# Flamingo block with experts and butterflies: full-precision products for the shared expert and the last projections, in place of split operands

## The chip, the cores and the metric

The kernel runs on one core of a Trainium2 chip. The metric is the device time of one execution in microseconds (us). The engines of the core are named as in the profile: PE (TensorE; PEld is its weight load), ACT (ScalarE), DVE (VectorE), POOL (GpSimd) and SP (SyncE, which here only issues transfers).

## The reference

Four residual layers on x, 4 x 1024 tokens of 256 features, float32. Each reads a layer norm of x and adds tanh(gate) times its result.

```python
x = x + tanh(g_xattn[0]) * cross_attention(layernorm(x), ctx, Wq, Wk, Wv, Wo)   # 16 heads, stablemax
x = x + tanh(g_ffn[0])   * experts(layernorm(x), ...)
x = x + tanh(g_xattn[1]) * attention(layernorm(x), ctx, ctx)                    # 16 heads, softmax
x = x + tanh(g_ffn[1])   * butterfly_ffn(layernorm(x), ...)

# experts: 64 experts, top 8 of each token, and one shared expert that every token takes
gu = x @ shared_gate_up_w                                  # 256 -> 2 * 512
shared = silu(gu[:, :512]) * gu[:, 512:] @ shared_down_w   # 512 -> 256
shared = shared * sigmoid(x @ shared_gate_w)
...

# butterfly_ffn
h = x @ W_exp + b_exp                                      # 256 -> 1024
h = butterfly(h, up_weights)                               # 10 stages, linear
h = gelu(h + up_bias)
h = butterfly(h, down_weights)                             # 10 stages, linear
y = h @ W_con + b_con                                      # 1024 -> 256
```

## The kernel before

The tokens are taken in 8 halves of 512 (four tiles of 128). The program has three stages with a meeting of all engines between them. What each engine does, and in which order, comes from one list of units per stage (`plan_first`, `plan_experts`, `plan_last`); every engine walks the whole list and runs the part of each unit that it has, in that order and no other. Semaphores tie the parts together.

Stage 1 is the first attention with the router. It writes the normalised features of each half to DRAM (`feats_scratch`).

Stage 2 is `plan_experts` (line 240). It has a phase that builds the lists of tokens (32 tiles: DVE and ACT make one-hot rows in `hots`, PE sums them in `place`, L803), then a loop of 69 iterations over 64 experts: POOL gathers the tokens of expert n, PE turns those of n-3 (L817), makes gate and up of n-4 (L827) and down of n-5 (L836), and POOL scatters the result (L1663). Two side streams are fed in one step at a time. `fusing`, two steps per iteration, multiplies the butterfly stages into the weights before and behind them (L786, and `across`, which is 8 wide operations each of ACT and DVE, L1078 and L1445). `back` is the shared expert: one step after every second tile from tile 5 on (14 steps), three behind the list phase, and one per iteration where n is no multiple of 8. A half of the shared expert is nine steps (`shared_steps`, line 212): load, split, four `sh_up` blocks with `sh_inner` beside them, a last `sh_inner`, two `sh_down` blocks. The first half has a tenth step, `sh_weights`.

Stage 3 is `plan_last`: the second attention of half h, beside it the softmax peaks of half h+1 (L856, L858, L1532) and the last layer of half h-1. This last layer comes in two bursts a half (`burst`, line 281): four `up` blocks (L908) with peaks between them, then four `out` blocks (L921), one per chunk of attention.

The shared expert and the last layer's two products are made of reduced-precision products (type fp32r), as many as a float32 needs: each operand is split into a rounded high part and a low part that is what is left, and three products are summed in PSUM: high x high, low x high, high x low (`PRODUCTS`). The splits are made by ACT (a copy that rounds) and DVE (a subtraction): of the weights once (`sh_weights`, `split_up`, `split_con`), of the features once a half (`sh_split`, `turn_f`), of the shared expert's inner values in each block (`sh_inner`, L1050 and L1416). The last layer's hidden values are rounded by DVE (L1580) and their rest is made by POOL (L1682). All other products of the kernel on float32 tiles, such as L628, L705, L827, L836 and L786, are single full-precision matmuls.

Of the kernel before, what the change touches and what calls it, by code (L numbers as in the profile page):

```python
# [8 lines left out]
F32 = mybir.dt.float32  # L9
F32R = mybir.dt.float32r  # L10
# [3 lines left out]
ALU = mybir.AluOpType  # L14
# [41 lines left out]
PRODUCTS = ((0, 0), (1, 0), (0, 1))  # L56
# [277 lines left out]
def plan_last():  # L334
# [5 lines left out]
    splits = [("split_up", q) for q in range(0, HB, 2)] + [("split_con", q) for q in (0, 4)]  # L340
# [4 lines left out]
    plan += [("peaks", 0)] + splits + [("scores1", 0)]  # L345
# [31 lines left out]
def build(nc, D, out):  # L377
    ctx = ExitStack()
    with ctx:
# [31 lines left out]
        with ExitStack() as scope:  # L411
            w_con = sb("w_con_fused", [P, HB, DIM], F32, scope)
        con_lo = sb("w_con_low", [P, HB, DIM], F32R)
# [47 lines left out]
        with ExitStack() as scope:  # L461
            w_up = sb("w_up_fused", [P, CD, HID], F32, scope)
        up_lo = sb("w_up_low", [P, CD, HID], F32R)
        hid_bias = sb("hidden_bias", [P, HB], F32)
        b_out = sb("bias_out", [P, DIM], F32)
        with ExitStack() as scope:
# [20 lines left out]
            w_sgu = s1("w_shared_up", [P, 2, CD * 2 * SHARED], F32R)  # L487
            w_sd = s1("w_shared_down", [P, 2, SK * DIM], F32R)
            sh_feats = s1("feats_m", [P, CD * HALF], F32)
            sh_parts = s1("feat_parts", [P, 2, CD * HALF], F32R)  # L490
            sh_silu = [s1(f"shared_silu{i}", [P, HALF], F32) for i in range(3)]
            sh_inner = s1("shared_inner", [P, 2, SK, HALF], F32R)
# [8 lines left out]
            staging = bf_v[:, :, :].rearrange("p a n -> p (a n)")  # L501


        with ExitStack() as scope:
            s2 = lambda n, s, d: sb(n, s, d, scope)
            up_hi = s2("w_up_high", [P, CD, HID], F32R)
            con_hi = s2("w_con_high", [P, HB, DIM], F32R)
            up_parts, con_parts = (up_hi, up_lo), (con_hi, con_lo)
# [13 lines left out]
            feats = s2("feats3", [P, 2, CD, HALF], F32R)  # L522
            hidden = [s2(f"hidden{i}", [P, 2, HALF], F32R) for i in range(BURST)]
            whole = [s2(f"hidden_whole{i}", [P, HALF], F32) for i in range(2)]
# [10 lines left out]
        sh_in, sd_in, con_in, expert_in = sem("sh_in"), sem("sd_in"), sem("con_in"), sems("expert_in", 8)  # L535
# [4 lines left out]
        pool_set, ln_var, ln_rstd, x_biased, x_added, out_biased, hid_split = (  # L540
            sem(n) for n in ("pool_set", "ln_var", "ln_rstd", "x_biased", "x_added", "out_biased", "hid_split"))
# [6 lines left out]
        sh_split, sh_mult, sh_inner_set, matrix_set, across_set = (  # L548
            sem(n) for n in ("sh_split", "sh_mult", "sh_inner_set", "matrix_set", "across_set"))
        x_first, x_att, hid_cast, con_split, out_added = (  # L550
            sem(n) for n in ("x_first", "x_att", "hid_cast", "con_split", "out_added"))
# [3 lines left out]
        feats_set, hot_a_set, got_turned, silu_set, sh_silu_set, sh_rounded, part_set, across_own = (  # L555
            sem(n) for n in ("feats_set", "hot_a_set", "got_turned", "silu_set", "sh_silu_set", "sh_rounded", "part_set", "across_own"))
# [17 lines left out]
        def tensor_program(T):  # L574
# [181 lines left out]
            def sh_down(h, two):  # L756
                key = ("sh_down", h, two)
                if two == 0:
                    T.wait_ge(sh_inner_set, SK * (h + 1))
                    if h == 0:  # L760
                        T.wait_ge(sh_split, 4)
# [1257 lines left out]
```

## Time and profile before

| | before |
|---|---|
| median of 3 runs | 1429.22 us (1424.58 to 1436.71) |
| the profiled execution | 1429.54 us |
| its span | 1427.9 us |
| mean granted PE clock | 0.891 |
| busy: PE, PEld | 80%, 57% of the span |
| busy: DVE, ACT, POOL | 57%, 52%, 26% of the span |
| chain that ended last | PE 59%, DVE 20%, ACT 8% |

The span runs from the first to the last instruction; 1.6 us of the execution lie outside it. In this execution stage 2 begins at about 457 us and stage 3 at about 860 us. Busy shares are means over the three stages, and a busy PE may be one that only keeps its pipeline filled. The chain that ended last is followed back from the last instruction, at each step to what released it.

### The profile page before, as it was taken

How to read it: one execution, taken by the hardware profiler on the slowest of the kernel's cores; microseconds unless marked ns; L12 is line 12 of the kernel's file. 1: busy time of each engine (PE TensorE's matmuls, PEld its weight loads, DVE VectorE, ACT ScalarE, POOL GpSimd, SP SyncE). 2: the span in 40 equal slices, each digit the busy share in tenths (PEclk: the TensorE clock that was granted, in tenths of full speed). 3: DMA queues.
4: the chain of work that ended last, by engine and by line, in shares of the span. 5: the costliest groups of instructions: out<-in, count | busy, mean ns of one | idle time of the engine just before them, and what ended most of it. 6: DMA issues, size and time to landing. Idle time of an engine off the chain costs nothing.

```text
span 1427.9 us, 18301 instructions
## 1 busy us (share of the span) xinstructions
PE 1140.4 (80%) x6049; PEld 820.0 (57%) x6049; DVE 814.5 (57%) x2036; ACT 747.8 (52%) x1471; POOL 373.4 (26%) x320
## 2 busy tenths in 40 slices
PE   4788878887884767999689980778887889788897
PEld 4353543543433556888678870545665657566666
DVE  4386587677774554554654543664556645655543
ACT  2686677677881653555655531233435444543452
POOL 2011011011000001466546662103132423312223
PEclk9697898998896898999999995577999999999998
DMA  8324414414202302577657745302123040311000
GB/s 246 83 63 118 115 60 118 136 38 118 78 34 84 126 1 90 121 181 179 173 131 174 189 88 144 98 24 70 45 69 108 1 113 2 107 28 33 18 15 15
DMA packets 89899, 129.76 MB, mean 91 GB/s; under 512 B 20496, under 2 KB 59792, under 8 KB 89552
## 3 DMA queue, kind: packets, MB, share of 16 engines
q1 hardware_dynamic: 77520, 109.73, 25.9%
q0 software_dynamic: 12288, 18.88, 7.6%
q8 instruction: 49, 0.80, 0.2%
q14 instruction: 42, 0.34, 0.1%
HBM read 72.18 MB, written 30.70 MB: 72 GB/s over the span
## 4 chain that ended last, share of the span: by engine, by line
PE 59%; DVE 20%; ACT 8%; issue 4%; DMA 4%; SPq 3%; POOL 0%; POOLq 0%; DVEq 0%; ACTq 0%
PE psum L921 6%; PE psum L751 6%; PE psum L908 5%; PE psum L662 4%; PE psum L657 4%; PE psum L827 4%; PE psum L639 4%; PE psum L767 3%; PE psum L786 3%; SPq L1739 3%; PE psum L856 3%; PE psum L836 2%; PE psum L628 2%; DVE weights L1292 2%; DVE stats L1191 2%
## 5 line engine op out<-in xcount | busy, mean ns | idle before, releaser
L639 PE MATMUL psum<-q_stack,k_stack 96*128 96x512 f32 (+1 forms) x256 | 139.1, 558 | 62.8 <-DVE weights L1292 28.4
L1630 POOL TENSOR_SCALAR vareps<-moments 128x4 f32<-128x4 f32 x32 | 7.5, 234 | 621.1 <-DVE moments L1194 621.1
L1532 DVE TENSOR_REDUCE peaks<-psum 128x2 f32<-128x308 f32 x256 | 108.7, 469 | 54.9 <-PE psum L858 54.8
L856 PE MATMUL psum<-k_stack,q_stack 96*128 96x256 f32 x256 | 93.3, 416 | 47.6 <-DMA q_stack<-q_stage 22.2
L1663 POOL DMA_INDIRECT expert_sums<-made,sum_rows x64 | 102.0, 1593 | 103.3 <-DVE made L1502 88.0
L639 PEld LDWEIGHTS psum<-q_stack,k_stack 96*128 96x128 f32 (+1 forms) x256 | 54.2, 216 | 119.5 <-DVE weights L1292 44.8
L662 PE MATMUL psum<-weights,values 128*32 128x512 f32 x512 | 109.4, 713 | 8.6 <-DVE weights L1292 8.6
L1135 ACT ACTIVATE weights<-psum 128x512 f32<-128x512 f32 x160 | 92.0, 595 | 38.6 <-PE psum L639 32.4
L1292 DVE SCALAR_TENSOR_TENSOR weights<-psum,weights 128x512 f32<-128x512 f32 x160 | 107.0, 679 | 5.3 <-ACT weights L993 4.8
L1682 POOL TENSOR_TENSOR hidden<-hidden_whole,hidden 128x512 fp32r<-128x512 f32 x64 | 82.1, 1282 | 105.8 <-DVE hidden L1580 105.8
L1655 POOL DMA_INDIRECT got<-rows_scratch,tokens x64 | 68.9, 1076 | 142.5 <-DVE sum_rows L1489 123.4
L993 ACT ACTIVATE weights<-weights 128x512 f32<-128x512 f32 x160 | 101.2, 632 | 1.1
L921 PE MATMUL psum<-w_con_high,hidden 128*128 128x256 f32 x512 | 101.6, 298 | 0.0
L988 ACT ACTIVATE weights<-weights 128x512 f32<-128x512 f32 x160 | 100.4, 628 | 0.0
L751 PE MATMUL psum<-feat_parts,w_shared_up 128*128 128x512 f32 x384 | 98.4, 406 | 0.0
L856 PEld LDWEIGHTS psum<-k_stack,q_stack 96*128 96x128 f32 x256 | 56.3, 220 | 72.3 <-issue 25.5
L908 PE MATMUL psum<-feats,w_up_high 128*128 128x512 f32 x256 | 83.5, 419 | 11.6 <-ACT hidden_whole L1163 5.9
L921 PEld LDWEIGHTS psum<-w_con_high,hidden 128*128 128x128 f32 x512 | 80.2, 189 | 14.9 <-issue 7.9
L657 PE MATMUL psum<-weights,values 128*128 128x512 f32 x128 | 82.3, 730 | 3.2 <-DVE weights L1292 3.1
L1580 DVE CAST hidden<-hidden_whole 128x512 fp32r<-128x512 f32 x64 | 45.9, 717 | 66.1 <-ACT hidden_whole L1163 65.8
L980 ACT ACTIVATE weights<-psum 128x512 f32<-128x512 f32 x128 | 75.8, 592 | 12.4 <-PE psum L639 7.4
L751 PEld LDWEIGHTS psum<-feat_parts,w_shared_up 128*128 128x128 f32 x384 | 71.8, 194 | 14.4
(187 smaller groups left out, 2617.0 us busy)
## 6 DMA issues: line engine op xcount, KB each, us to landing
q_stack<-q_stage SPq DMA_DIRECT2D x192, 128.0 KB, 2.4
expert_w<-in_expert_w SPq DMA_DIRECT2D x64, 384.0 KB, 3.8
expert_sums<-zeros SPq DMA_DIRECT2D x6, 1408.0 KB, 7.1
fetched<-expert_sums SPq DMA_DIRECT2D x16, 512.0 KB, 4.8
wk_stack<-in_wk SPq DMA_DIRECT2D x16, 384.0 KB, 3.9
rows_scratch<-rows SPq DMA_DIRECT2D x8, 640.0 KB, 3.4
k_raw<-in_k SPq DMA_DIRECT2D x16, 300.0 KB
x<-in_x SPq DMA_DIRECT2D x8, 512.0 KB, 6.1
```

The costliest lines, as they stand in the source:

```text
L639: T.matmul(to, k[0:row, head, :], q[0:row, head // 2, :], start=True, stop=True).then_inc(scored, 1)
L657: T.matmul(to, vals[:, 1, 4 * g:4 * g + 4, :], w[(n + 4) % len(w)][:, :], start=False, stop=True).then_inc(weighed, 1)
L662: m = T.matmul(to[32 * j:32 * j + 32, :], vals[:, 0, 4 * g + j, :], w[(n + j) % len(w)][:, :], start=True, stop=False, tile_position=(0, 3 ...
L751: m = T.matmul(misc.ap(key, half), w_sgu[:, pw, a:a + P], sh_parts[:, pf, c * HALF:(c + 1) * HALF], start=n == 0 and c == 0, stop=n == 2 a ...
L856: T.matmul(view[:, :, 0:P], q[0:STACK, p, t * P:(t + 1) * P], keys[0:STACK, 2 * p:2 * p + 2, :], start=True, stop=True)
L908: m = T.matmul(wide.ap(key), up_parts[pw][:, c, k * P:(k + 1) * P], feats[:, pf, c, :], start=i == 0 and c == 0, stop=i == 2 and c == CD - 1)
L921: m = T.matmul(out_bank[t // 2][:, t % 2 * DIM:(t % 2 + 1) * DIM], hidden[k][:, ph, t * P:(t + 1) * P], con_parts[pw][:, BURST * b + k, :] ...
L988: A.activation(weights[n % 9][:, :], weights[n % 9][:, :], ACT.Ln, bias=1.0, scale=1.0 if on_act else -1.0).then_inc(logged, 1)
L993: A.activation(weights[n % 9][:, :], weights[n % 9][:, :], ACT.Exp, scale=-1.0).then_inc(exped, 1)
L1292: V.scalar_tensor_tensor(weights[n % 9][:, :], score_bank[n % 5], 1.0, weights[n % 9][:, :], ALU.add, ALU.max).then_inc(weighted, 1)
L1532: V.tensor_reduce(peaks[h % 2][:, t, 2 * p:2 * p + 2], view, AX.X, ALU.max).then_inc(wide.frees(key, i), 1)
L1663: G.indirect_dma_start(sum_dram[e % SUMS], bass.IndirectOffsetOnAxis(ap=sum_rows[:, e:e + 1], axis=0), made[e % 4][:, :], None, bounds_che ...
```

## The change

Each group of three reduced-precision products becomes one float32 product: in `sh_up` and `sh_down` (shared expert) and in `up` and `out` (last layer). All splits go, with their tiles and semaphores. The weights of the shared expert are loaded into their own tiles. Features and inner values of the shared expert have two buffers each. `turn_f` is shared out: ACT copies the first 128 features, DVE the others. `gelu` writes straight to `hidden`, and ACT now waits itself until the `out` block of the burst before has read that tile. A half of the shared expert is six steps (seven for the first) where it was nine; the rule that feeds the steps is as it was, so the steps come at other places.

```diff
 def shared_steps(h):
-    steps = [[("sh_load", h)]]
-    if h == 0:
-        steps.append([("sh_weights",)])
-    steps.append([("sh_split", h)])
-    steps.append([("sh_up", h, 0)])
-    steps += [[("sh_inner", h, k), ("sh_up", h, k + 1)] for k in range(SK - 1)]
-    return steps + [[("sh_inner", h, SK - 1)]] + [[("sh_down", h, two)] for two in range(HT // 2)]
+    steps = [[("sh_load", h)]] if h == 0 else []
+    steps += [[("sh_up", h, k)] for k in range(SK)]
+    if h + 1 < HALVES:
+        steps[-SK].append(("sh_load", h + 1))
+    return steps + [[("sh_down", h, two)] for two in range(HT // 2)]
...
-    plan += [("peaks", 0)] + splits + [("scores1", 0)]
+    plan += [("peaks", 0), ("scores1", 0)]
...
             def sh_up(h, k):
                 key = ("sh_up", h, k)
                 if k == 0:
-                    T.wait_ge(sh_split, 4 + h if h else 3)
+                    T.wait_ge(sh_in[h % 2], 16 * (h // 2 + 1))
+                    if h == 0:
+                        T.wait_ge(sgu_in, 16)
                 for half in range(2):
                     T.wait_ge(*misc.vacant(key, half))
-                    for n, (pw, pf) in enumerate(PRODUCTS):
-                        for c in range(CD):
-                            a = c * 2 * SHARED + half * SHARED + k * P
-                            m = T.matmul(misc.ap(key, half), w_sgu[:, pw, a:a + P],
-                                         sh_parts[:, pf, c * HALF:(c + 1) * HALF],
-                                         start=n == 0 and c == 0, stop=n == 2 and c == CD - 1)
+                    for c in range(CD):
+                        a = c * 2 * SHARED + half * SHARED + k * P
+                        m = T.matmul(misc.ap(key, half), w_sgu[:, a:a + P], sh_feats[h % 2][:, c * HALF:(c + 1) * HALF],
+                                     start=c == 0, stop=c == CD - 1)
                     m.then_inc(misc.fills(key, half), 1)
...
-                        for n, (pi, pw) in enumerate(PRODUCTS):
-                            m = T.matmul(misc.ap(key)[:, i * DIM:(i + 1) * DIM], sh_inner[:, pi, k, t * P:(t + 1) * P],
-                                         w_sd[:, pw, k * DIM:(k + 1) * DIM], start=k == 0 and n == 0,
-                                         stop=k == SK - 1 and n == 2)
+                        m = T.matmul(misc.ap(key)[:, i * DIM:(i + 1) * DIM], sh_inner[h % 2][:, k, t * P:(t + 1) * P],
+                                     w_sd[:, k * DIM:(k + 1) * DIM], start=k == 0, stop=k == SK - 1)
...
-                for i, (pw, pf) in enumerate(PRODUCTS):
-                    for c in range(CD):
-                        m = T.matmul(wide.ap(key), up_parts[pw][:, c, k * P:(k + 1) * P], feats[:, pf, c, :],
-                                     start=i == 0 and c == 0, stop=i == 2 and c == CD - 1)
+                for c in range(CD):
+                    m = T.matmul(wide.ap(key), w_up[:, c, k * P:(k + 1) * P], feats[:, c, :],
+                                 start=c == 0, stop=c == CD - 1)
...
             def out_part(h, b, k):
                 n = BURST * (2 * h + b) + k
-                if h == 0 and k == 0:
-                    T.wait_ge(con_split, 4 + b + 1)
-                T.wait_ge(hid_split, n + 1)
+                T.wait_ge(*wide.freed(("up", h, BURST * b + k)))
                 for t in range(HT):
                     if k == 0 and t % 2 == 0 and n:
                         T.wait_ge(out_added, n // BURST * 2 - 1 + t // 2)
-                    for q, (ph, pw) in enumerate(PRODUCTS):
-                        m = T.matmul(out_bank[t // 2][:, t % 2 * DIM:(t % 2 + 1) * DIM],
-                                     hidden[k][:, ph, t * P:(t + 1) * P], con_parts[pw][:, BURST * b + k, :],
...
+                    m = T.matmul(out_bank[t // 2][:, t % 2 * DIM:(t % 2 + 1) * DIM], hidden[k][:, t * P:(t + 1) * P],
+                                 w_con[:, BURST * b + k, :], start=k == 0 and t % 2 == 0,
...
             def turn_f(h):
                 if h:
                     A.wait_ge(*wide.filled(("up", h - 1, HB - 1)))
-                for c in range(CD):
-                    evacuate(wide, ("turn_f", h), feats[:, 0, c, :], c).then_inc(feats_rounded, 1)
+                evacuate(wide, ("turn_f", h), feats[:, 0, :], 0).then_inc(wide.frees(("turn_f", h), 0), 1)
 
             def up(h, k):
-                n, key = HB * h + k, ("up", h, k)
-                if n >= 2:
-                    A.wait_ge(hid_split, n - 1)
+                key, b = ("up", h, k), (2 * h + k // BURST) - 1
+                if b >= 0:
+                    A.wait_ge(out_made, BURST * b + k % BURST + 1)
                 A.wait_ge(*wide.filled(key))
-                A.activation(whole[n % 2][:, :], wide.ap(key), ACT.Gelu,
+                A.activation(hidden[k % BURST][:, :], wide.ap(key), ACT.Gelu,
...
-                V.tensor_tensor(sh_silu[n % 3][:, :], sh_silu[n % 3][:, :], misc.ap(key, 1),
+                V.tensor_tensor(sh_inner[h % 2][:, k, :], sh_silu[n % 3][:, :], misc.ap(key, 1),
                                 ALU.mult).then_inc(misc.frees(key, 1), 1)
...
-                V.tensor_copy(hidden[k % BURST][:, 0, :], whole[n % 2][:, :]).then_inc(hid_cast, 1)
+                if h:
+                    V.wait_ge(*wide.filled(("up", h - 1, HB - 1)))
+                V.wait_ge(*wide.filled(key, 1))
+                V.tensor_copy(feats[:, 1, :], wide.ap(key, 1)).then_inc(wide.frees(key, 1), 1)
...
-            def hidden_rest(h, k):
-                n = HB * h + k
-                G.wait_ge(hid_cast, n + 1)
-                G.tensor_tensor(hidden[k % BURST][:, 1, :], whole[n % 2][:, :], hidden[k % BURST][:, 0, :].bitcast(F32),
-                                ALU.subtract).then_inc(hid_split, 1)
...
             def sh_load(h):
-                if h:
-                    S.wait_ge(sh_split, 3 + h if h > 1 else 3)
-                S.dma_start(sh_feats[:, :], feats_dram[h]).then_inc(sh_in, 16)
+                if h >= 2:
+                    S.wait_ge(*misc.filled(("sh_up", h - 2, SK - 1), 1))
+                S.dma_start(sh_feats[h % 2][:, :], feats_dram[h]).then_inc(sh_in[h % 2], 16)
```

Where the steps come now. On PE, the end of stage 2's list phase before the change, from the last two `sh_down` blocks of the first half (L767) to the product that turns the lists (L810); L803 is a tile's one-hot sum (8 matmuls each) and L751 is `sh_up`:

```order
L767 MATMUL psum<-w_shared_down,shared_inner 128x256 x24
L803 MATMUL psum<-hot_b,hot_a 128x256 x48
L751 MATMUL psum<-feat_parts,w_shared_up 128x512 x12
L803 MATMUL psum<-hot_b,hot_a 128x256 x16
L751 MATMUL psum<-feat_parts,w_shared_up 128x512 x12
L803 MATMUL psum<-hot_b,hot_a 128x256 x16
L751 MATMUL psum<-feat_parts,w_shared_up 128x512 x24
L767 MATMUL psum<-w_shared_down,shared_inner 128x256 x24
L810 MATMUL psum<-ident,by_expert 128x64
```

And the same place after the change (L784 is the one-hot sum, L735 `sh_up`, L749 `sh_down`, L791 the turned lists), from the second half's last `sh_up`:

```order
L735 MATMUL psum<-feats_m,w_shared_up 128x512 x4
L784 MATMUL psum<-hot_b,hot_a 128x256 x16
L749 MATMUL psum<-w_shared_down,shared_inner 128x256 x8
L784 MATMUL psum<-hot_b,hot_a 128x256 x16
L749 MATMUL psum<-w_shared_down,shared_inner 128x256 x8
L784 MATMUL psum<-hot_b,hot_a 128x256 x16
L735 MATMUL psum<-feats_m,w_shared_up 128x512 x4
L784 MATMUL psum<-hot_b,hot_a 128x256 x16
L735 MATMUL psum<-feats_m,w_shared_up 128x512 x12
L749 MATMUL psum<-w_shared_down,shared_inner 128x256 x8
L791 MATMUL psum<-ident,by_expert 128x64
```

Before the lists are turned PE now has 12 `sh_up` and 5 `sh_down` blocks to do, where it had 8 and 3. The first of them stands behind six tiles, where it stood behind ten.

On PE in the expert loop, the last `sh_down` block before the change (L767), close to the loop's end; L817, L836 and L827 are the turn, down, and gate and up of three experts:

```order
L827 MATMUL psum<-got_t,expert_w 128x128 x4
L767 MATMUL psum<-w_shared_down,shared_inner 128x256 x24
L817 MATMUL psum<-ident,got 128x128 x2
L786 MATMUL psum<-w_con_fused,stage_m 128x256
L836 MATMUL psum<-expert_w,inner 128x256
L786 MATMUL psum<-w_con_fused,stage_m 128x256
L827 MATMUL psum<-got_t,expert_w 128x128 x4
L817 MATMUL psum<-ident,got 128x128 x2
L836 MATMUL psum<-expert_w,inner 128x256
```

The last one after the change (L749; L808, L798, L817 and L767 are the lines of gate and up, turn, down, and fusing):

```order
L808 MATMUL psum<-got_t,expert_w 128x128 x4
L749 MATMUL psum<-w_shared_down,shared_inner 128x256 x8
L798 MATMUL psum<-ident,got 128x128 x2
L767 MATMUL psum<-w_con_fused,stage_m 128x256
L817 MATMUL psum<-expert_w,inner 128x256
L767 MATMUL psum<-w_con_fused,stage_m 128x256
L808 MATMUL psum<-got_t,expert_w 128x128 x4
L798 MATMUL psum<-ident,got 128x128 x2
```

Behind it the gate and up products of 32 experts follow with nothing of the shared expert between them; before, those of 5. Inside the loop there are 31 iterations with a block of the shared expert, where there were 37.

## Rows read from the trace of the kernel before

**Rows 1.** The page's head: busy us (share of the span) xinstructions.
```profile
span 1427.9 us, 18301 instructions
PE 1140.4 (80%) x6049; PEld 820.0 (57%) x6049; DVE 814.5 (57%) x2036; ACT 747.8 (52%) x1471; POOL 373.4 (26%) x320
```

**Rows 2.** Busy time by stretch: stretch, its us, each engine's busy us, granted clock, DMA.
```profile
451.40:564.10 112.70, 72.46 (x441) 55.99 (x442) 58.80 (x129) 54.20 (x89) 0.00 (x0) 0.86 0.22 77
580.00:680.00 100.00, 98.54 (x593) 85.73 (x592) 50.74 (x125) 57.15 (x163) 62.55 (x47) 1.00 0.73 174
680.00:740.00 60.00, 44.58 (x253) 38.28 (x252) 36.27 (x89) 36.04 (x93) 28.67 (x22) 0.89 0.56 143
...
1060.00:1186.40 126.40, 106.28 (x620) 79.23 (x616) 73.71 (x174) 56.00 (x86) 39.63 (x30) 0.96 0.23 63
```

**Rows 3.** The chain that ended last, in order of time: start, us, what.
```profile
246.69 1.73 PE psum L628 x4
256.07 1.73 PE psum L705 x8
...
590.46 2.75 PE psum L751 x12
...
606.59 2.88 PE psum L767 x24
...
1371.24 5.57 PE psum L908 x24
...
1417.88 5.70 PE psum L921 x48
```

**Rows 4.** PE in the list phase: start, us, engine line operation, [idle before <-releaser].
```profile
462.02 9.36 PE L803 MATMUL psum<-hot_b,hot_a 128*128 128x256 bf16 x56 [8.21 <-ACT hot_a L1094]
...
490.21 2.99 PE L751 MATMUL psum<-feat_parts,w_shared_up 128*128 128x512 f32 x12
...
495.73 1.05 PE L803 MATMUL psum<-hot_b,hot_a 128*128 128x256 bf16 x8 [1.63 <-ACT hot_a L1094]
496.53 3.02 PE L751 MATMUL psum<-feat_parts,w_shared_up 128*128 128x512 f32 x12
...
513.25 3.11 PE L767 MATMUL psum<-w_shared_down,shared_inner 128*128 128x256 f32 x24
...
519.80 3.11 PE L767 MATMUL psum<-w_shared_down,shared_inner 128*128 128x256 f32 x24
...
547.80 5.72 PE L751 MATMUL psum<-feat_parts,w_shared_up 128*128 128x512 f32 x24
...
561.25 0.27 PE L810 MATMUL psum<-ident,by_expert 64*128 64x64 f32 x1
```

**Rows 5.** POOL's scatters in the expert loop, in order of time.
```profile
585.47 1.60 POOL L1663 DMA_INDIRECT expert_sums<-made,sum_rows  x1 [2.15 <-DVE made L1502]
...
590.69 1.58 POOL L1663 DMA_INDIRECT expert_sums<-made,sum_rows  x1 [2.27 <-DVE made L1502]
...
761.83 1.59 POOL L1663 DMA_INDIRECT expert_sums<-made,sum_rows  x1 [0.31 <-issue]
...
765.14 1.59 POOL L1663 DMA_INDIRECT expert_sums<-made,sum_rows  x1 [0.31 <-issue]
...
853.54 1.55 POOL L1663 DMA_INDIRECT expert_sums<-made,sum_rows  x1 [0.53 <-issue]
855.95 1.55 POOL L1663 DMA_INDIRECT expert_sums<-made,sum_rows  x1 [0.86 <-DVE made L1502]
```

**Rows 6.** The costliest groups: count, busy us, mean ns, idle before them.
```profile
L1682 POOL TENSOR_TENSOR hidden<-hidden_whole,hidden 128x512 fp32r<-128x512 f32 x64 | 82.1, 1282 | 105.8 <-DVE hidden L1580 105.8
L1580 DVE CAST hidden<-hidden_whole 128x512 fp32r<-128x512 f32 x64 | 45.9, 717 | 66.1 <-ACT hidden_whole L1163 65.8
```

**Rows 7.** The timeline of an up burst, PE and ACT.
```profile
1139.63 0.69 ACT L1163 ACTIVATE hidden_whole<-psum,hidden_bias 128x512 f32<-128x512 f32 x1 [1.81 <-PE psum L908]
1140.37 0.73 PE L908 MATMUL psum<-feats,w_up_high 128*128 128x512 f32 x2 [0.27 <-ACT hidden_whole L1163]
```

More of the change, by code:

```diff
@@ L458, in build @@
             pos_i = s0("pos_i", [P, 2, HT, EXPERTS], I32)
[L461 to L463 removed]
+        w_up = sb("w_up_fused", [P, CD, HID], F32)
         hid_bias = sb("hidden_bias", [P, HB], F32)
@@ L486, in build @@
             made = [s1(f"made{i}", [P, DIM], F32) for i in range(4)]
[L487 to L490, printed above, removed]
+            w_sgu = s1("w_shared_up", [P, CD * 2 * SHARED], F32)
+            w_sd = s1("w_shared_down", [P, SK * DIM], F32)
+            sh_feats = [s1(f"feats_m{i}", [P, CD * HALF], F32) for i in range(2)]
             sh_silu = [s1(f"shared_silu{i}", [P, HALF], F32) for i in range(3)]
-            sh_inner = s1("shared_inner", [P, 2, SK, HALF], F32R)
+            sh_inner = [s1(f"shared_inner{i}", [P, SK, HALF], F32) for i in range(2)]
             bf_u = s1("butterfly_u", [P, HB, DIM + 1], F32)
@@ L521, in build @@
             peak_t = s2("peak_t", [HEADS, 2, HALF], F32R)
-            feats = s2("feats3", [P, 2, CD, HALF], F32R)
-            hidden = [s2(f"hidden{i}", [P, 2, HALF], F32R) for i in range(BURST)]
-            whole = [s2(f"hidden_whole{i}", [P, HALF], F32) for i in range(2)]
+            feats = s2("feats3", [P, CD, HALF], F32)
+            hidden = [s2(f"hidden{i}", [P, HALF], F32) for i in range(BURST)]
         stage_over = sem("stage_over")
@@ L758, in sh_down @@
                 if two == 0:
-                    T.wait_ge(sh_inner_set, SK * (h + 1))
+                    T.wait_ge(*misc.freed(("sh_up", h, SK - 1), 1))
                     if h == 0:
-                        T.wait_ge(sh_split, 4)
+                        T.wait_ge(sd_in, 16)
                 T.wait_ge(*misc.vacant(key))
@@ L1040, in sh_up @@
                 if n >= 3:
-                    A.wait_ge(sh_inner_set, n - 2)
+                    A.wait_ge(*misc.freed(("sh_up", (n - 3) // SK, (n - 3) % SK), 1))
                 A.wait_ge(*misc.filled(key, 0))
                 A.activation(sh_silu[n % 3][:, :], misc.ap(key, 0), ACT.Silu).then_inc(misc.frees(key, 0), 1)
-            def sh_inner_(h, k):
-                n = SK * h + k
-                if h and k == 0:
-                    A.wait_ge(*misc.filled(("sh_down", h - 1, 1)))
-                A.wait_ge(*misc.freed(("sh_up", h, k), 1))
-                A.activation(sh_inner[:, 0, k, :], sh_silu[n % 3][:, :], ACT.Copy).then_inc(sh_rounded, 1)
             def stage_matrix(n):
@@ L1170, in scalar_program @@
                      "exp": exp, "weigh": weigh, "turn_att": turn_att, "turn_rows": turn_rows, "gate": gate,
-                     "sh_weights": sh_weights, "sh_split": sh_split_, "sh_up": sh_up, "sh_inner": sh_inner_,
+                     "sh_up": sh_up,
                      "matrix": stage_matrix, "inside": inside, "across": across, "turn_up": turn_up,
@@ L1597, in vector_program @@
                      "normalize": normalize, "project_o": project_o, "gate": gate, "top": top_, "pick": pick,
-                     "count": count, "sh_weights": sh_weights, "sh_split": sh_split_, "sh_up": sh_up,
-                     "sh_inner": sh_inner_, "sh_down": sh_down, "matrix": stage_matrix, "across": across,
+                     "count": count, "sh_up": sh_up, "sh_down": sh_down, "matrix": stage_matrix, "across": across,
                      "hid_bias": set_hid_bias, "out_bias": set_out_bias, "hots": hots, "lists": set_lists,
@@ L1602, in vector_program @@
                      "key_split1": key_split1, "turn_q1": turn_q1, "peak": peak, "peaks": turn_peaks,
-                     "normalize1": normalize1, "split_up": split_up, "split_con": split_con,
-                     "turn_f": turn_f, "up": up, "out": out_add}
+                     "normalize1": normalize1, "turn_f": turn_f, "out": out_add}
             for n, plan in enumerate((first, experts, last)):
```

102 lines of the change are left out of this document (15 added, 87 removed).

## The prediction

> **What bounds the kernel now.** I read the page's head, then the busy time by stretch, then the chain of waits in order of time, and last the timeline of the places that change. PE is busy for 1140.4 of 1427.9 us [rows 1], and in the expert loop for 98.54 of 100 us [rows 2]: there nothing else sets the time. It has slack where the butterflies are scaled by ACT and DVE (44.58 of 60 us busy), in the list phase (72.46 of 112.70) and in the last stage (106.28 of 126.40) [rows 2]. So the first question is what the change does to PE's own time, the second where that time lies beside a wait.
>
> **The price of a product.** A float32 product leaves two records in the trace. L628 makes two products of 512 columns at a time: four records, 1.73 us, so 0.865 us each; L705 makes four of 256 columns: eight records, 1.73 us, 0.433 us each [rows 3]. Both are at the full clock. The reduced products, from the same rows: a block of `sh_up` is 12 in 2.75 us, of `sh_down` 24 in 2.88 us, four `up` blocks are 24 in 5.57 us (1.39 a block), four `out` blocks 48 in 5.70 us (1.425 a block) [rows 3]. In place of these a block has 4, 8, 2 and 4 float32 products: 4 x 0.865 = 3.46, 8 x 0.433 = 3.46, 1.73 and 1.73 us. The change makes each block longer:
> - `sh_up` by 0.71 us, 32 blocks: 22.7 us
> - `sh_down` by 0.58 us, 16 blocks: 9.3 us
> - `up` by 0.34 us, 64 blocks: 21.8 us
> - `out` by 0.305 us, 64 blocks: 19.5 us
>
> That is 73.3 us more of PE. What is three products on paper is dearer as one: a reduced product of 512 columns takes 0.23 us, the float32 one close to four times that, and only at 256 columns (0.12 against 0.433, 3.6 times) does the weight load narrow the gap.
>
> A rule of the Trainium skill stands beside this (FP8 and Floating Point Precision, TensorE Precision Notes): a true float32 product is four passes through the array. By that page's rule, with each pass at the price of a reduced product, the sum would be an estimated 105 us (rival 5); L628 and L705 say 73.
>
> **What the change takes away.** On ACT and DVE the splits: in stage 2 the weights' and the features', and `sh_inner` in each of 32 blocks; in stage 3 the weights', the second step of `turn_f`, and 64 casts of DVE (45.9 us, mean 717 ns) with 64 subtractions of POOL (82.1 us) [rows 6]. Where PE is full this is worth nothing. I go through the stages.
>
> *Stage 1* is untouched: 0.
>
> *List phase.* Here PE waits for ACT's one-hot rows: 1.63 us ahead of the tile's sums at 495.73, and the pitch of a step (two tiles and an `sh_up` block) is 496.53 - 490.21 = 6.32 us; of a step with `sh_down` 519.80 - 513.25 = 6.55 us [rows 4]. The wait is a ring: DVE multiplies the block's result, only then makes the next one-hot row, ACT scales it, PE sums it and starts the next block. The block is in this ring and the removed split is not, so the pitches become 6.32 + 0.71 = 7.03 and 6.55 + 0.58 = 7.13 us. Before, 9 of the 14 steps held a block; now all 14 do (10 `sh_up`, 4 `sh_down`). The first can start when about seven tiles are done, 462.02 + 9.36 = 471.4 [rows 4]. The clock is low there (0.86 over the stretch [rows 2]), for which I add one block's 3.4 us. The last of the 14 starts at 471.4 + 3.4 + 9 x 7.03 + 4 x 7.13 = 566.6 and ends at 570.0. Behind it stand two `sh_up` blocks, DVE's product and `sh_down` (11.2 us): the lists are turned at 581.2, in place of 561.25 [rows 4]. Term: +20 us. Bounds: +13 (the first steps at full clock, one us given back per half by the missing splits) to +23.
>
> *Expert loop.* The pitch of an iteration with `sh_up` is 590.69 - 585.47 = 5.22 us, all PE; without a block POOL's scatter and gather set it, 765.14 - 761.83 = 3.31; the last scatters come 2.41 apart [rows 5]. Before, 37 of 69 iterations had a block; now 31 have (pitch 5.9), all in the first 36, since nine steps a half are now six and the steps are handed out as fast as ever. Behind them are 29 iterations at 3.31 and 4 at 2.41: 105.6 us. The 31 take 182.9. For the five that remain, the first gathers, and the scaling in 680 to 740, where PE is idle for 15.4 us [rows 2] of which the blocks now beside it cover about half, I take 18. Sum 306.5, against the 296.3 from 561.25 to the last scatter's end at 857.5. Term: +10 us; bounds 0 (all idle at the scaling covered) to +30 (rival 2).
>
> *Last stage.* A burst beside peaks has the ring `up`, gelu, next `up`: 0.69 us of ACT at 1139.63, and PE starts at 1140.37 as it ends [rows 7]. Three of four `up` blocks lie on it, the other under DVE; the four `out` blocks follow each other. Per half that is 6 x 0.34 + 8 x 0.305 = 4.5 us. The cast and POOL's subtraction run beside the next block and save nothing there. `turn_f` on two engines takes one DVE step of about 0.7 us off the path. So +3.8 us for six halves, 22.8. The last two halves have bursts without peaks, in which PE is full: 16 x 0.34 + 16 x 0.305 - 1.4 = 8.9, and 1 for the low clock at the very end. Term: +33 us; bounds +22 (the removed casts, whose mean lies 0.29 above the 0.43 of a free one, give back 0.2 a block) to +41, all of PE's.
>
> New waits: ACT's gelu waits for the `out` block of the burst before, five chunks earlier, and SP's feature load for a block of two halves before; both are long done, cost 0, and what is queued behind them is not held. Removed splits at the start of stage 3 lie under the transfer of the peaks: 0.
>
> Sum: 1429.5 + 20 + 10 + 33 = 1492.5 us, against the profiled execution; the median of the runs, 1429.2, is 0.3 less, so 1492.
>
> **The rivals.**
> 1. *PE's whole 73 us lands, and the idle stays* (1429.5 + 73 = 1503). For it: PE is nearly full where most blocks are. Against: fewer low-clock stretches, `turn_f`, the scaling. Chance 0.17.
> 2. *The late half of the expert loop is bound by transfers.* DMA is busy for 73% of the time there [rows 2], at (855.95 - 585.47) / 62 = 4.36 us an expert [rows 5]: 3.2 us each. At a pitch of 3.31 that is 96%, more than any stretch of [rows 2] shows. At 80% the pitch is 4.0: 29 x 0.69 = +20, 1512. Against: the pitch of 3.31 exists, if only for single iterations. Chance 0.12.
> 3. *The conversions were worth more than they look.* ACT and DVE are in-order, and a split ahead of a one-hot row or a peak delays PE. If half of stage 3's `up` increments and two thirds of the list phase's hide behind that: 1429.5 + 7 + 5 + 20 = 1462. Chance 0.13.
> 4. *Faster: PE's idle swallows the longer blocks.* PE is idle for 40.2 us in the list phase, 15.4 at the scaling and 10 in each half of the last stage [rows 2]. If the longer blocks lie in it and the removed conversions (12 us ahead of the first `sh_up`, one cast or subtraction per burst) come back as 27 us, the time is 1402. It decides once more than 46 of the 73 us are hidden. Against it: 98.54 of 100, and that the rings above hold the blocks themselves. Chance 0.03.
> 5. *A fourth product at full price*: each of the 640 products costs one reduced product and its weight load more, 256 x 0.229 + 384 x 0.12 = 105 us: 1429.5 + 105 = 1534. Against it L628 and L705, which are such products. Chance 0.02. This is the case in which the Trainium skill's four passes (same section) would each cost what a reduced one does; the trace does not agree.
> 6. The change does nothing to the time, because fewer instructions offset longer ones: within 1%, chance 0.02.
>
> The forecast keeps 0.51. Range: from the lower bounds of the terms (13 + 0 + 22 = 35, 1465) to rival 2's 1512; outside lie most of rival 3, 4, 5 and 6, some 0.17. The measurement of this kernel can tell about 1% from no change. Slower by over 1% is everything but 4 and 6: 0.95; within 1% 0.02; faster 0.03.
>
> **What would show it.** PE busy near 1140 + 73 = 1213 us with 640 records fewer than 6049 (1,920 reduced ones go, 2 x 640 come). `sh_up` blocks of 3.46 us and `up` blocks of 1.73. The lists turned near 581 us, the last scatter near 888, and in the 100 us before it scatters 3.3 us apart with PE idle in between. A half of the last stage in 67 us, where it took 63.2 (half of the stretch 1060 to 1186.4 [rows 2]). It would be wrong if float32 products at these places took other than 0.865 and 0.433 us, if the list phase's pitch stayed at 6.3, or if the late scatters came 4.0 apart.

## The result and the profile after

The changed kernel takes 1491.14 us (median of 4 runs, 1483.18 to 1492.66), the kernel before 1428.39 us (1424.58 to 1436.71): ratio 1.042, 95% interval 1.036 to 1.0479. It is 4.2% slower; 1492 us had been forecast. The page's head and the stretches of the profile after, in the columns of [rows 1, 2]; the stretches are the list phase, the expert loop, its last 92 us, and one stretch of the last stage as long as that of [rows 2]:

```profile
span 1488.2 us, 16704 instructions
PE 1197.5 (80%) x5409; PEld 774.2 (52%) x5409; DVE 727.7 (49%) x1915; ACT 714.0 (48%) x1414; POOL 290.5 (20%) x256
```
```profile
462.90:586.00 123.10, 94.42 (x433) 58.20 (x433) 42.72 (x86) 45.84 (x77) 0.00 (x0) 0.95 0.17 62
586.00:891.60 305.60, 273.98 (x1346) 205.32 (x1345) 125.46 (x340) 143.60 (x422) 170.08 (x128) 0.97 0.60 148
800.00:891.60 91.60, 70.88 (x414) 57.85 (x414) 34.23 (x102) 44.94 (x143) 71.55 (x54) 0.96 0.77 175
...
1050.00:1176.40 126.40, 109.52 (x504) 71.56 (x503) 60.73 (x152) 52.82 (x82) 19.03 (x14) 0.96 0.23 63
```

PE has 640 records fewer and 57.1 us more to do; ACT, DVE and POOL have 34, 87 and 83 us less, and the kernel is slower all the same. In the last 92 us of the loop PE is idle for 20.7 us.

The chain of waits gives the price of the new blocks (start, us, what), beside [rows 3]:

```profile
598.75 3.43 PE psum L735 x8
...
615.85 3.46 PE psum L749 x16
...
1470.12 6.87 PE psum L886 x16
1476.98 6.92 PE psum L896 x32
```

`sh_up` 3.43, `sh_down` 3.46, `up` 6.87 / 4 = 1.72, `out` 6.92 / 4 = 1.73 us: each within 0.03 us of what L628 and L705 had said. The timeline of PE in the list phase, as in [rows 4], from its first sums on:

```profile
462.90 8.18 PE L784 MATMUL psum<-hot_b,hot_a 128*128 128x256 bf16 x48 [8.31 <-ACT hot_a L1045]
476.91 6.08 PE L735 MATMUL psum<-feats_m,w_shared_up 128*128 128x512 f32 x8 [5.83 <-DMA feats_m<-feats_scratch]
...
486.39 3.60 PE L735 MATMUL psum<-feats_m,w_shared_up 128*128 128x512 f32 x8
489.83 1.04 PE L784 MATMUL psum<-hot_b,hot_a 128*128 128x256 bf16 x8
492.51 1.05 PE L784 MATMUL psum<-hot_b,hot_a 128*128 128x256 bf16 x8 [1.65 <-ACT hot_a L1045]
493.39 3.60 PE L735 MATMUL psum<-feats_m,w_shared_up 128*128 128x512 f32 x8
...
507.40 3.62 PE L749 MATMUL psum<-w_shared_down,shared_inner 128*128 128x256 f32 x16
...
514.54 3.62 PE L749 MATMUL psum<-w_shared_down,shared_inner 128*128 128x256 f32 x16
...
585.97 0.28 PE L791 MATMUL psum<-ident,by_expert 64*128 64x64 f32 x1
```

The pitch is 493.39 - 486.39 = 7.00 us with `sh_up` and 514.54 - 507.40 = 7.14 with `sh_down`; PE still waits 1.65 us for ACT in each step, as before. The first block waits until 476.91 for the transfer of its features, which SP had issued at about 466, behind the stage's other loads. POOL's scatters late in the loop, as in [rows 5]:

```profile
850.10 1.59 POOL L1566 DMA_INDIRECT expert_sums<-made,sum_rows  x1 [0.31 <-issue]
...
853.35 1.59 POOL L1566 DMA_INDIRECT expert_sums<-made,sum_rows  x1 [0.31 <-issue]
...
890.08 1.55 POOL L1566 DMA_INDIRECT expert_sums<-made,sum_rows  x1 [1.12 <-DVE made L1425]
```

The first two are 3.25 us apart, and between them POOL is idle only for the issues between its instructions (1.59 + 1.05 us of work and two issues of 0.30 to 0.31). PE meanwhile waits for gathered tokens: 13.2 us in 16 waits between 560 and 880. So POOL sets the pace where no block is left for PE.

### The profile page after: what moved, and what is told of

Read it like the earlier page. It is cut to its first block, busy times and chain, and to the rows that moved or that the text cites. A ratio compares the mean times of both kernels' runs of the same rounds, so it can differ in the third digit from the quotient of the medians.

```text
span 1488.2 us, 16704 instructions
## 1 busy us (share of the span) xinstructions
PE 1197.5 (80%) x5409; PEld 774.2 (52%) x5409; DVE 727.7 (49%) x1915; ACT 714.0 (48%) x1414; POOL 290.5 (20%) x256
## 4 chain that ended last, share of the span: by engine, by line
PE 56%; DVE 17%; ACT 7%; DMA 6%; issue 5%; SPq 5%; POOL 2%; POOLq 0%; DVEq 0%; ACTq 0%
PE psum L735 7%; PE psum L896 7%; PE psum L886 7%; PE psum L645 4%; SPq L1636 4%; PE psum L749 4%; PE psum L640 3%; PE psum L622 3%; PE psum L808 2%; PE psum L837 2%; PE psum L767 2%; PE psum L611 2%; DVE stats L1134 2%; DVE weights L1235 2%; PE psum L565 2%
## 5 line engine op out<-in xcount | busy, mean ns | idle before, releaser
L837 PE MATMUL psum<-k_stack,q_stack 96*128 96x256 f32 x256 | 108.9, 482 | 41.4 <-DMA q_stack<-q_stage 22.1
L886 PE MATMUL psum<-feats,w_up_fused 128*128 128x512 f32 x256 | 123.8, 619 | 12.2 <-ACT hidden L1106 9.2
L735 PE MATMUL psum<-feats_m,w_shared_up 128*128 128x512 f32 x256 | 117.8, 605 | 5.8 <-DMA feats_m<-feats_scratch 5.8
L896 PE MATMUL psum<-w_con_fused,hidden 128*128 128x256 f32 x512 | 121.8, 382 | 0.0
L896 PEld LDWEIGHTS psum<-w_con_fused,hidden 128*128 128x128 f32 x512 | 95.1, 190 | 26.6 <-issue 15.4
L640 PE MATMUL psum<-weights,values 128*128 128x512 f32 x128 | 78.2, 696 | 3.1 <-DVE weights L1235 3.1
L886 PEld LDWEIGHTS psum<-feats,w_up_fused 128*128 128x128 f32 x256 | 46.9, 194 | 63.7 <-issue 44.0
L1106 ACT ACTIVATE hidden<-psum,hidden_bias 128x512 f32<-128x512 f32 x64 | 43.0, 686 | 74.9 <-PE psum L886 74.7
L735 PEld LDWEIGHTS psum<-feats_m,w_shared_up 128*128 128x128 f32 x256 | 47.8, 196 | 54.9 <-issue 48.6
```

Of the source, the lines that this page charges most:

```text
L640: T.matmul(to, vals[:, 1, 4 * g:4 * g + 4, :], w[(n + 4) % len(w)][:, :], start=False, stop=True).then_inc(weighed, 1)
L735: m = T.matmul(misc.ap(key, half), w_sgu[:, a:a + P], sh_feats[h % 2][:, c * HALF:(c + 1) * HALF], start=c == 0, stop=c == CD - 1)
L837: T.matmul(view[:, :, 0:P], q[0:STACK, p, t * P:(t + 1) * P], keys[0:STACK, 2 * p:2 * p + 2, :], start=True, stop=True)
L886: m = T.matmul(wide.ap(key), w_up[:, c, k * P:(k + 1) * P], feats[:, c, :], start=c == 0, stop=c == CD - 1)
L896: m = T.matmul(out_bank[t // 2][:, t % 2 * DIM:(t % 2 + 1) * DIM], hidden[k][:, t * P:(t + 1) * P], w_con[:, BURST * b + k, :], start=k == ...
```

## The experiments

Three marks, which each trace shows in one row, cut a span into four pieces: the first sums of the one-hot rows (462.90 above), the lists turned (585.97), and the last scatter's end (890.08 + 1.55). The piece ahead of the first mark is the same code in all kernels. In us; the pieces are of the profiled execution:

| kernel | before the lists | list phase | expert loop | last stage | median of runs | ratio to before, 95% |
|---|---|---|---|---|---|---|
| before | 462.0 | 99.2 | 296.2 | 570.4 | 1428.4 | |
| changed | 462.9 | 123.1 | 305.7 | 596.6 | 1491.1 | 1.0360 to 1.0479 |
| e1 shared expert only | 459.4 | 123.1 | 305.9 | 577.1 | 1463.3 | 1.0165 to 1.0267 |
| e2 last projections only | 461.7 | 99.2 | 296.4 | 599.3 | 1458.6 | 1.0149 to 1.0245 |
| e3 four reduced products | 459.8 | 110.0 | 328.6 | 620.9 | 1520.8 | 1.0558 to 1.0672 |
| e4 changed, respaced | 464.2 | 123.1 | 292.8 | 602.6 | 1478.9 | 1.0260 to 1.0385 |
| e5 changed, rows ahead | 462.0 | 96.9 | 306.1 | 599.0 | 1469.0 | 1.0250 to 1.0305 |
| e6 before, rows ahead | 458.9 | 81.8 | 296.6 | 576.9 | 1414.5 | 0.9863 to 0.9913 |
| e7 conversions kept | 459.6 | 106.2 | 315.2 | 606.8 | 1488.9 | 1.0383 to 1.0438 |
| e8 before, filled | 458.6 | 81.8 | 298.7 | 575.1 | 1414.5 | 0.9833 to 0.9934 |
| e9 changed, old pacing | 455.8 | 90.0 | 315.0 | 600.5 | 1468.6 | 1.0239 to 1.0307 |
| e10 changed, both | 457.4 | 99.2 | 294.3 | 598.0 | 1453.0 | 1.0129 to 1.0222 |
| e11 before, two queues | 458.4 | 81.9 | 296.0 | 567.6 | 1411.8 | 0.9841 to 0.9929 |

The list phase and the loop repeat within 0.6 us where the code is the same, with two exceptions: e5 and e10 have one list phase, 96.9 and 99.2, and e4 and e10 one loop, 292.8 and 294.3. The piece before the lists is one code and spreads over 8.4 us (455.8 to 464.2). The last stage spreads over 7 us (570.4, 577.1, 576.9, 575.1 for one code) and, with the new products, over 6 us (596.6, 599.3, 602.6, 599.0, 600.5, 598.0), so there a single profile tells no small difference; the two means are 24.5 us apart. The kernel before had a median of 1432.3 beside e1 to e4, 1429.4 beside e5 to e8 and 1429.9 beside e9 to e11.

**The halves of the change by themselves.** e1 takes only the changes of stage 2, e2 only those of stage 3.

> Only the shared expert of stage 2 is changed; the last projections keep their splits and three reduced products. Theory (PE's longer blocks land where they stand, stage by stage): the last scatter ends where it does in the changed kernel, near 891 us instead of 857.5, and the last stage takes as long as before: 1428.4 + 34 = 1462 us (1458 to 1467). Rival (the two halves of the change lean on each other, for instance through the clock or through what the removed conversions free): the time is more than 8 us from 1462. The terms of the prediction said +30, 1458.

> Only the last projections of stage 3 are changed; the shared expert keeps its splits and three reduced products. Theory from the two traces: the start of the stage 2.8 us shorter, five halves 3.3 us longer each, the last two halves 9.9 us, the first burst 2.6 us: +26, so 1454.5 us (1450 to 1459). The term of the prediction said +33, 1461. Rival (what stage 3 saves was owed to the changed stage 2): 1461 or more. Together with the run of the shared expert alone the increments should add up to the 62.7 us of the whole change.

Measured +31.0 and +26.3 us over the before that ran beside them, 57.3 together; the whole change is +62.7, and the intervals (e1's and e2's are 14 us wide each) cover the 5.4 us between. The pieces of e1 agree with the changed kernel's to 0.2 us in stage 2, those of e2 with the kernel before. So the halves are independent in stage 2 and, as far as the spread tells, in the last stage, and neither is worth having.

**The price of the product.** e3 adds the fourth reduced product:

```
-PRODUCTS = ((0, 0), (1, 0), (0, 1))
+PRODUCTS = ((0, 0), (1, 0), (0, 1), (1, 1))
```

> The kernel before with a fourth reduced product (low by low) in each of the four projections, all splits kept. By the rows of before each of 256 products of 512 columns adds 0.229 us and each of 384 of 256 columns 0.12 us: PE +105 us (sh_up blocks 3.67 us, sh_down 3.84, up 1.84, out 1.90). Theory (a float32 product is cheaper than four reduced ones, 0.865 against 0.92 and 0.433 against 0.48): 1518 to 1535 us, 25 to 45 us slower than the changed kernel. Rival (a float32 product is the same work as four reduced ones, and the changed kernel only has the conversions less): within 15 us of the changed kernel's 1491.

Its chain of waits:

```profile
602.65 3.66 PE psum L751 x16
614.40 3.83 PE psum L767 x32
...
1500.00 7.42 PE psum L908 x32
1507.43 7.53 PE psum L921 x64
```

3.66, 3.83, 1.86 and 1.88 us a block: a float32 product costs 94% (3.43 / 3.66) of four reduced ones at 512 columns and 90% (3.46 / 3.83) at 256. The time is 88.5 us over before, inside the theory's range; rival 5 had put 105 us on the float32 products, and even with four reduced ones only 88.5 of them reach the time.

e7 is the kernel before with every split and wait, and one float32 product of the high parts (the low parts are computed and not summed):

```
-PRODUCTS = ((0, 0), (1, 0), (0, 1))
+PRODUCTS = ((0, 0),)
...
-up_parts[pw][:, c, k * P:(k + 1) * P], feats[:, pf, c, :],
+up_parts[pw][:, c, k * P:(k + 1) * P].bitcast(F32), feats[:, pf, c, :].bitcast(F32),
```

> The kernel before with all its splits and waits, but one float32 product of the rounded high parts in place of the three reduced ones (the low parts are computed and left out of the sums). PE has the price of the changed kernel, everything else is of the kernel before; what separates it from the changed kernel is the worth of the removed conversions and the shorter list of steps. Theory (in stage 3 the start gains 2.8 us and turn_f about 0.7 to 1.0 a half, some 10 us; in stage 2 the blocks are only handed out differently, within 8 us): 1493 to 1510 us, so the conversions were worth 5 to 20 us. Rival 3 of the prediction (conversions worth some 30 us and more of the path): 1520 or more. Rival (worth nothing): 1488 to 1493.

1488.9 us, where the changed kernel has 1491.1: taken by itself this was the rival "worth nothing". But the pieces differ: the list phase is 16.9 us shorter than the changed kernel's, the loop 9.5 longer, the last stage 10.2 longer (by e7's 606.8 against the six values above, 4.2 to 10.2). Two effects had to be hidden in one total, so e9 gives the changed kernel the old pacing, with empty steps between the blocks:

```
-    steps = [[("sh_load", h)]] if h == 0 else []
+    steps = [[("sh_load", h)], [], []] if h == 0 else [[], []]
...
-    return steps + [[("sh_down", h, two)] for two in range(HT // 2)]
+    return steps + [[]] + [[("sh_down", h, two)] for two in range(HT // 2)]
```

> The changed kernel with the empty steps of the kernel before put back between the shared expert's blocks (73 steps again, 11 blocks in the list phase, 37 in the expert loop), nothing else. Theory (the kernel with kept conversions ended its loop at 881 us against 891.7 of the changed one, because the shortened list of steps runs out of blocks in the loop's late half): the last scatter ends near 881 us, the last stage takes 596 as in the changed kernel, the time is 1476 to 1484 us. Rival (the 10 us come from elsewhere, for instance the features' load or the clock): 1487 to 1495.

1468.6 us, 22.5 less than the changed kernel and 7.4 below the range that I expected. The theory named the wrong place: the gain was to come in the loop, but the loop is 9.3 us longer than the changed kernel's (315.0 and 305.7), because it holds 37 blocks and not 31. The list phase is 33.1 us shorter (90.0 and 123.1), because it holds 11 blocks and not 17. A block in the list phase costs some 5.5 us, for it stands in the ring; in the loop it costs about 1.5, for it partly fills time in which PE would wait for POOL.

The loop is as long as e7's (315.2), with the same blocks at the same places. The list phase is not: 106.2 us in e7. What stands there in e7, PE's timeline:

```profile
472.88 3.21 PE L803 MATMUL psum<-hot_b,hot_a 128*128 128x256 bf16 x16 [3.97 <-ACT hot_a L1094]
479.02 1.89 PE L803 MATMUL psum<-hot_b,hot_a 128*128 128x256 bf16 x8 [2.94 <-ACT hot_a L1094]
480.70 4.44 PE L751 MATMUL psum<-feat_parts,w_shared_up 128*128 128x512 f32 x8
...
514.08 4.82 PE L767 MATMUL psum<-w_shared_down,shared_inner 128*128 128x256 f32 x16
...
560.46 5.41 PE L767 MATMUL psum<-w_shared_down,shared_inner 128*128 128x256 f32 x16 [2.58 <-DVE shared_inner L1416]
```

and in e9:

```profile
455.84 12.76 PE L784 MATMUL psum<-hot_b,hot_a 128*128 128x256 bf16 x80 [8.17 <-ACT hot_a L1045]
470.32 3.70 PE L735 MATMUL psum<-feats_m,w_shared_up 128*128 128x512 f32 x8 [1.71 <-DMA feats_m<-feats_scratch]
...
541.76 3.72 PE L749 MATMUL psum<-w_shared_down,shared_inner 128*128 128x256 f32 x16 [0.85 <-DVE shared_inner L1339]
```

In e7 the splits of weights and features stand ahead of the one-hot rows on ACT and DVE, PE waits 3.97 and 2.94 us, and the first block starts 21.1 us after the phase did; in e9 ten tiles go through in one piece and the block starts after 14.5. That is 6.6 of the 16.2 us. Another 3.6 come through the clock: three blocks of e7 behind waits for the one-hot rows or for DVE, at granted clocks of 0.80, 0.73 and 0.68, take 4.44, 4.82 and 5.41 us, where the same three take 3.62 to 3.72 in e9 at 1.00. The rest, some 6 us, I did not divide further. The four kernels divide the whole change:
- price of the product, before to e7: 1488.9 - 1429.4 = +59.5 us
- conversions, with the buffers and waits that the change renews along with them, e7 to e9: 1468.6 - 1488.9 = -20.3 us. The profiled executions are 26.5 us apart: 16.2 in the list phase, 0.2 in the loop, 6.3 in the last stage, which that stage's spread doesn't secure, and 3.8 ahead of the list phase, where the code is the same.
- fewer steps handed out at the old pace, e9 to the changed kernel: 1491.1 - 1468.6 = +22.5 us, in pieces +33.1 in the list phase and -9.3 in the loop

**The pacing.** e4 hands the blocks out in every second iteration of the loop.

```
-            if other and (other is fusing or n % 8):
+            if other and (other is fusing or n % 2):
```

> The changed kernel with the shared expert's steps handed out in every second iteration of the expert loop instead of seven of eight, so that blocks stand in its late half too. Theory (late iterations without a block are held by POOL's gather and scatter at 3.25 us while PE needs 2.41, so PE idles for most of 31.7 us of the loop): pairs of iterations need 2 x 2.41 + 3.44 = 8.26 us of PE, above POOL's 6.5, the loop's idle falls from 31.7 to 10 to 18 us, and the time to 1470 to 1478 us. Rival (the loop is bound by the transfers of the experts' weights, or the idle moves to the scaling of the butterflies, where the blocks now stand beside it): 1485 to 1495.

The loop is 12.9 us shorter (305.7 to 292.8), and 11.8 shorter between e5 and e10. The median, 1478.9 beside a before of 1432.3, is just above the theory's range; by itself the total would not settle it, since the ratio's interval overlaps the changed kernel's. PE by stretch, the loop, its scaling and its late half:

```profile
587.50:880.10 292.60, 268.58 (x1345) 201.16 (x1344) 126.11 (x340) 142.45 (x422) 171.65 (x128) 0.99 0.65 154
...
700.00:760.00 60.00, 49.08 (x244) 35.94 (x243) 35.16 (x91) 37.29 (x99) 32.47 (x24) 0.97 0.65 164
780.00:870.00 90.00, 86.79 (x451) 66.97 (x450) 35.56 (x97) 41.33 (x127) 56.65 (x43) 1.00 0.64 145
```

PE is busy for 86.79 of 90 us late in the loop (75.01 in the same stretch of the changed kernel), and the 13.2 us of waits for gathered tokens are gone: the late idle was a lack of blocks, as the theory said. Part of it comes back at the scaling, where PE is now idle for 10.9 of 60 us; in the changed kernel it was idle for 3.0 between 700 and 760.

**The ring in the list phase.** e5 makes the one-hot rows two tiles ahead, in the same three buffers; e6 does the same to the kernel before.

```
-    plan.append(("hots", 0))
+    plan += [("hots", 0), ("hots", 1)]
...
-        if i + 1 < TILES:
-            plan.append(("hots", i + 1))
+        if i + 2 < TILES:
+            plan.append(("hots", i + 2))
```

> The changed kernel with the one-hot rows of the list phase made two tiles ahead in place of one (same buffers, same work). Theory (the step's pitch of 7.01 us is the ring block, DVE's product, one-hot rows, ACT's scaling, PE's sums): with rows ready before the block ends, a step is the block and two tiles of sums, 3.44 + 1.8 = 5.24 us, and 13 steps give back 1.75 us each: the lists are turned near 563 us instead of 586, the time is 1464 to 1472 us. Rival (PE's 1.65 us of waiting per step has another source, the banks or the clock): no change, 1487 to 1495.

> The kernel before with the one-hot rows made two tiles ahead. Theory (the same ring, with blocks in 9 of 13 steps; a step with a block falls from 6.32 to 2.75 + 1.8 = 4.55 us): 13 to 22 us faster than before, 1410 to 1419 us. Rival (the splits of weights, features and inner values on ACT and DVE now set the pitch, since they stand in the same queues): less than 8 us faster, 1424 or more.

Both came out: 1469.0 (22 us less) and 1414.5 us (14.9 less than before beside it, ratio 0.9888). PE in the list phase of e5:

```profile
491.99 3.60 PE L735 MATMUL psum<-feats_m,w_shared_up 128*128 128x512 f32 x8
495.43 1.91 PE L784 MATMUL psum<-hot_b,hot_a 128*128 128x256 bf16 x16
497.18 3.62 PE L749 MATMUL psum<-w_shared_down,shared_inner 128*128 128x256 f32 x16
```

The wait for ACT is gone and the pitch is 5.19 us (497.18 - 491.99) in place of 7.00. The ring that the prediction drew was there, and it was in the order of the instructions, not in the work: DVE's product of the block stood ahead of rows that could have been made while PE ran the block. e6 beats both kernels: its interval, 0.9863 to 0.9913, lies below 1.

> The changed kernel with the one-hot rows two tiles ahead and the shared expert's steps in every second iteration. If the two gains stand in different places they add: 22 us in the list phase and 12 to 16 in the loop, 1491 - 36 = 1455 us (1450 to 1460), still 1 to 2% slower than the kernel before and 40 us behind the kernel before with its rows ahead. Rival (they share one reserve): 1462 or more.

e10 puts e4 and e5 together: 1453.0 us, as added up. The best float32 version that I have is still 1.3 to 2.2% slower than before, and 38.5 us behind e6. The old pacing of e9 together with the rows ahead was not run; by the pieces it could be the better float32 version.

**Two tries at more.** e8 gives e6's loop two steps in each iteration of the scaling and fewer elsewhere; e11 lets POOL issue 4 of the 12 loads of a half's queries in the last stage.

> The kernel of e6 with the shared expert's steps handed out in two of three iterations, and two at a time in the eight iterations in which ACT and DVE scale the butterflies (iterations 28 to 35). Theory (of 27 us in which PE idles in the expert loop 15 lie at the scaling and blocks can stand there): the loop gets 5 to 12 us shorter than in e6. Rival (iterations without a block are held by POOL at 3.3 us, so the idle only moves to them): within 4 us of e6.

> The kernel before with its one-hot rows two tiles ahead, and in the last stage 4 of the 12 loads of the queries' stack issued by GpSimd in place of SyncE. The chain of waits of before and after shows the 12 issues one behind the other, 0.64 us each, ahead of the next half's first peak. Theory (the issue on one queue is on the path): 8 issues in place of 12, 2.6 us less in each of the halves where PE waits there, 10 to 17 us less than the 1414.5 of the rows-ahead kernel: 1398 to 1405. Rival (GpSimd's own issues take longer than what SyncE saves, or hold its other work): 1412 or more.

e8 gained nothing (1414.5, loop 298.7 against 296.6): the rival held. e11 has 1411.8 us, 2.7 less than e6, with intervals that overlap: inconclusive, and the 10 us that I expected are not there. The waits of PE that I meant to shorten did not shrink in sum. In e6 PE waits for the queries' stack ahead of the peaks in three halves, 3.68, 3.71 and 3.69 us; in e11 in four, 3.06, 2.21, 3.04 and 3.04. I had priced the issues and not the waits.

## Why the prediction was right, step by step

- *PE's price.* Blocks of 3.46, 3.46, 1.73 and 1.73 us were forecast, 3.43, 3.46, 1.72 and 1.73 came. That it is the weight load that narrows the gap at 256 columns, no run separates. PE's busy time rose by 57.1 us and not by 73. Of the 16 us, 3.8 lie ahead of the list phase, where the code is the same (351.8 us busy before, 348.0 after), 3 in stage 2 and 9 in the last stage (449.0 to 481.1, where 41 more had been forecast). Part is how busy time is counted: in the list phase a block's record went from 2.99 [rows 4] to 3.60 us, +0.61, while the pitch rose by 0.68. The granted clock also rose, from 0.86 to 0.87 ahead of the list phase and from 0.87 to 0.89 in the last stage, and the products that did not change are shorter for it; how much of the 9 that is, no run shows.
- *List phase, +20: measured +23.8*, just outside the upper bound of 23. The pitches (7.03 and 7.13) were right to 0.03 us. The first block was to start at 471.4, 9.4 us after the phase's first sums; it started 14.0 after them, at 476.91, because it waited for the transfer of its features, a wait that I had put at nothing. Its low clock cost less than I had added (6.08 us for the block, not 6.9). 4.6 - 0.8 is the whole miss of the phase; the lists were turned at 585.97, forecast 581.2, and the other 0.9 us lie ahead of the phase.
- *Expert loop, +10: measured +9.4* (305.66 against 296.25). Scatters 3.25 apart late in the loop, the last one near 888 forecast, 891.6 measured. Rival 2, transfers that hold the late half at a pitch of 4.0, failed: DMA was busy for 77% there and the pitch stayed 3.25. The scaling was covered better than by half: PE was idle for 3.0 us between 700 and 760, where it had been idle for 15.4 [rows 2]; so some other term of that sum was too small; which one I did not separate.
- *Last stage, +33: measured +26.2.* This term was mis-sized. A half takes 66.7 us (ACT loads the table of the gelu at the same place of three halves at 1108.26, 1175.07 and 1241.73), forecast 67. The lines below are the chain of waits in such a burst, beside [rows 7]: the `up` blocks start 1178.23 - 1175.41 = 2.82 us apart, 0.33 more than before (1135.38 to 1137.87), as forecast. Over the five halves from 1042.07 to 1374.53 a half is 3.3 us longer (66.49, before 316.15 / 5 = 63.23), 0.5 less than the 3.8 of the sum: 2.7 us. The other 3.9 lie ahead of 1042.07: from the last scatter's end to there the stage takes 150.4 us, before 150.5, where I had counted a sixth half at +3.8. The removed splits may have given that back, for I had put them at 0 under the transfer of the peaks, and the first gelu comes 2.3 us sooner after the last scatter (126.6 against 128.9). But for one code that time is 125.5 to 129.9 us in six kernels, and e7, which keeps the splits, has 127.9. So it is not shown. The last two halves, +9.9, came out as forecast.

```profile
1175.41 2.00 PE psum L886 x4
...
1177.49 0.70 ACT hidden L1106
1178.18 0.04 issue
1178.23 2.00 PE psum L886 x4
```

- *The sum* was 1492.5 for a profile of 1489.8: the terms were off by +0.9 ahead of stage 2's lists, +3.3 in stage 2 and -6.8 in the last stage. The errors have opposite signs. It is partly luck that the total is off by only 2.7 us.
- *What the terms did not show.* I wrote that the conversions were worth nothing where PE is full, and that is so (loop 315.0 and 315.2). But of the +20 of the list phase I moved the first block up by the splits' time and let all 14 steps hold blocks, and never named the two apart. They are 20.3 us of gain and 22.5 of loss, which all but cancel. Rival 3 was right in its mechanism: conversions ahead of one-hot rows do delay PE, by up to 16 us. It failed as a forecast because the same edit shortened the list of steps. Rival 1 ("the whole 73 lands") is refuted too: of the price alone 59.5 us landed.
- *Four passes.* The Trainium skill (FP8 and Floating Point Precision, TensorE Precision Notes) counts four passes for true float32. In e3 four reduced products take 7 to 11% longer than one float32 product, so the price of a float32 product is near that of four passes, and no run here counts the passes themselves; at the full price of a reduced product each, rival 5, the count does not fit.

## What to carry to other kernels

Price a change of precision by the record of a product of the same shape and type elsewhere in the trace: two rows gave all four blocks to 0.03 us. When an edit also deletes steps from a list that is handed out at a fixed pace, cost the new spacing as a change of its own, for it can be as large as what was deleted. And where PE waits for the same producer in every step, look first for a consumer's result that stands ahead of that producer's next work in its queue: the order of one unit in the list was worth 15 us in one kernel here and 22 in the other, with no work removed.

## What the runs showed of the hardware that I had not expected

- At the full clock a float32 product is not as dear as four reduced ones: 3.43 against 3.66 us for a block of four at 512 columns, 3.46 against 3.83 for eight at 256.
- Where POOL does nothing but gather and scatter, a pair takes 3.24 to 3.42 us, most often 3.25 or 3.31, in every kernel, also with DMA busy for 77% of the stretch.
- Four loads issued by POOL took 2.20 us, 0.55 each, where SyncE needs 0.64 us each; but SyncE's own eight then took 6.50 us, 0.81 each, and POOL's loads landed 4.0 us after their issue, SyncE's 2.5 (medians, e11).
